# A vision tower's last layer and first patch blocks as whole fp32 products on one Trainium2 core

## The reference, cut to what matters

```python
h = tok(x)                                   # patches @ W_lin.T + b, class token, positions
h = h + attention(layernorm(h))              # 16 heads of 64, relative position bias
h = h + moe(layernorm(h))                    # top 2 of 7 routed experts and a shared one, hidden 1024
# L1 attn: delta = sigmoid(s @ Wd.T + bd); value = s @ Wv.T + bv
#          state = (1 - delta) * state + delta * value, over the tokens
h = h + scan(layernorm(h))
# L1 ffn:  xr, xk = mixes of a token and the one before it
#          sigmoid(xr @ Wr) * (relu(xk @ Wk) ** 2 @ Wv)
h = h + rwkv_ffn(layernorm(h))
```

## Time and profile before

| | us |
|---|---|
| median of 3 runs (340.35 to 342.18) | 340.74 |
| the profiled execution's own time | 340.65 |
| its span | 338.6 |
| TensorE busy | 324.1 |
| VectorE busy | 216.9 |
| ScalarE busy | 197.8 |
| GpSimd busy | 144.5 |
| DMA, mean over the span | 131 GB/s |

### The profile page before, as it was taken

One profiled execution on the slowest core, in us unless ns is written; L12 is line 12 of the kernel. 1 busy time (PEld: TensorE's weight loads), 2 busy tenths in 40 slices (PEclk: granted clock), 3 DMA queues, 4 the chain that ended last, 5 costly groups with the idle time before them and its releaser, 6 DMA issues.

```text
span 338.6 us, 7784 instructions
## 1 busy us (share of the span) xinstructions
PE 324.1 (96%) x3308; PEld 304.6 (90%) x3308; DVE 216.9 (64%) x379; ACT 197.8 (58%) x332; POOL 144.5 (43%) x101
## 2 busy tenths in 40 slices
PE   8999999999999999999999989999999999989875
PEld 8976877899998999999999989999999999968765
DVE  2667233555564587678839685766757688736884
ACT  4772333755645685457687456656566566537681
POOL 3143012385442323548374365665665874000231
PEclk9999999999999999999999999999999999999999
DMA  7937450003000521568756456464758351000002
GB/s 275 407 124 221 136 200 0 6 2 128 4 2 4 186 64 65 188 204 282 220 184 189 120 212 208 153 214 155 217 162 293 135 155 53 1 5 2 1 0 73
DMA packets 30499, 44.43 MB, mean 131 GB/s; under 512 B 1586, under 2 KB 19314, under 8 KB 30332
## 3 DMA queue, kind: packets, MB, share of 16 engines
q1 hardware_dynamic: 27868, 39.89, 35.8%
q0 software_dynamic: 960, 2.43, 2.3%
q10 hardware_dynamic: 1632, 1.57, 1.4%
HBM read 38.22 MB, written 5.49 MB: 129 GB/s over the span
## 4 chain that ended last, share of the span: by engine, by line
PE 78%; DVE 11%; ACT 6%; issue 2%; DMA 1%; POOL 1%; ACTq 0%; SPq 0%; DVEq 0%
PE ps L1498 21%; PE ps L1500 20%; PE ps L1499 20%; DVE c_region L937 3%; PE ps L1530 3%; PE ps L1630 3%; PE ps L1657 2%; DVE w_lo L937 2%; PE ps L1523 2%; PE ps L1615 1%; DMA v_region<-in_patches 1%; ACT w_hi L637 1%; DVE s_region L1275 1%; DVE xn_lo L937 1%; PE ps L1547 1%
## 5 line engine op out<-in xcount | busy, mean ns | idle before, releaser
L1498 PE MATMUL ps<-c_region,w_hi 128*128 128x256 f32 (+2 forms) x320 | 95.2, 297 | 2.8 <-DVE c_region L937 1.5
L1500 PE MATMUL ps<-c_region,w_lo 128*128 128x256 f32 (+2 forms) x320 | 92.1, 288 | 0.0
L1499 PE MATMUL ps<-c_region,w_hi 128*128 128x256 f32 (+2 forms) x320 | 92.0, 288 | 0.0
L1498 PEld LDWEIGHTS ps<-c_region,w_hi 128*128 128x128 f32 x320 | 61.1, 191 | 4.5 <-DVE c_region L937 2.7
L402 POOL TENSOR_TENSOR w_lo<-w_stage,w_hi 128x1024 fp32r<-128x1024 f32 x15 | 44.7, 2981 | 45.1 <-ACT w_hi L637 45.0
L1499 PEld LDWEIGHTS ps<-c_region,w_hi 128*128 128x128 f32 x320 | 61.1, 191 | 0.2
L1500 PEld LDWEIGHTS ps<-c_region,w_lo 128*128 128x128 f32 x320 | 61.0, 191 | 0.0
L937 DVE TENSOR_TENSOR c_region<-s_region,c_region 128x512 fp32r<-128x512 f32 (+1 forms) x44 | 47.9, 1088 | 18.1 <-ACT c_region L772 12.6
L637 ACT ACTIVATE w_hi<-w_stage 128x1024 fp32r<-128x1024 f32 (+1 forms) x42 | 49.6, 1192 | 4.4 <-DVE v_region L1330 4.4
L1498 PE MATMUL ps<-xn_hi,w_hi 128*128 128x296 f32 x152 | 47.7, 314 | 1.1 <-DVE xn_lo L937 1.1
L1499 PE MATMUL ps<-xn_lo,w_hi 128*128 128x296 f32 x152 | 45.4, 299 | 0.0
(11 more groups left out here) (185 smaller groups left out, 637.1 us busy)
## 6 DMA issues: line engine op xcount, KB each, us to landing
w_stage<-in_w_gate SPq DMA_DIRECT2D x17, 512.0 KB, 4.2
w_stage<-in_w_up SPq DMA_DIRECT2D x17, 512.0 KB, 4.2
w_stage<-in_w_down SPq DMA_DIRECT2D x8, 1024.0 KB, 5.5
expert_rows<-zeros SPq DMA_DIRECT2D x1, 1792.0 KB, 13.8
v_region<-in_patches SPq DMA_DIRECT2D x3, 576.0 KB, 5.7
v_region<-expert_rows SPq DMA_DIRECT2D x1, 1536.0 KB, 7.2
expert_out<-v_region ACTq DMA_DIRECT2D x6, 256.0 KB, 3.9
v_region<-in_w_l SPq DMA_DIRECT2D x1, 1280.0 KB, 6.8
```

The lines of the kernel that those rows point to most:

```text
L1498: mm(o, a_h, b_h, start=start, stop=False)
L1499: mm(o, a_h, b_l, start=False, stop=False)
L1500: return mm(o, a_l, b_h, start=False, stop=stop)
```

## The change

- Patches and W_lin come as six blocks, one transfer each. Blocks 0 and 1 go to TensorE as they are, in one fp32 product instead of three; blocks 2 to 5 are split as before. TensorE begins with 5 zero products instead of 15.
- 16 of the 37 bias products stand between the mean and the variance of the first norm, 21 behind it. They use banks 5 and 7.
- `value(0, 0)` becomes `value_full(0, 0)`: two fp32 products of 512 columns. The load of w_o, which goes over w_v, waits for them.
- ScalarE casts w_k behind the first half's `high`, and w_q behind the second half's.
- `token_weights` and `choice_weights` stand behind expert 2's last copy.
- The last layers' weights are not split: they are loaded into the staging tile, and every product of those layers is one fp32 product (`full`). The casts and subtractions of their weights and inputs are gone.
- TensorE's list of the last layers stands within both branches (`last_layer`). 13 zero products are left out there (4, 7 and 2).

```diff
-            for i in range(3):
-                for o, x, n in ((wlin_s, w_lin, KF * D // 3), (patch_s, patches, PW // 3)):
-                    sp.dma_start(o[:, i * n:(i + 1) * n], x[:, i * n:(i + 1) * n]).then_inc(d_patch[i], 16)
+            for k in range(KF):
+                r = slice(k * FB, (k + 1) * FB)
+                sp.dma_start(vreg[:, r], blocks[:, r]).then_inc(d_patch[k], 16)
             sp.dma_start(pb[:], par).then_inc(s["d_par"], 16)
...
             sp.dma_start(part(2).rearrange("p (k n) -> p k n", k=HP), rows(w_o, HP)).then_inc(d_w[2], 16)
...
-            sp.wait_ge(s["xg_mm"], E - 1)
-            sp.dma_start(l1_s, w_l1).then_inc(s["d_l1"], 16)
+            sp.wait_ge(lo_e["g1"], NX)
+            sp.wait_ge(lo_e["u1"], NX)
+            sp.dma_start(pat(ws[:], L1AT[0], [HID, 4], [1, KD * D]),
+                         w_l1[:, 0:4 * KD * D].rearrange("p (i n) -> p i n", i=4)).then_inc(s["d_l1"], 16)
             reload("dn", NX, KH // 2)
+            sp.dma_start(ws[:, 2 * W1 + KH // 2 * D:2 * W1 + KH // 2 * D + KD * D],
+                         w_l1[:, 4 * KD * D:L1W]).then_inc(s["d_l1"], 16)
             for c in range(C):
                 sp.wait_ge(s["out_ok"] if c else s["out0_ok"], KD)
...
-            g.memset(zero[:], 0.0).then_inc(s["const_set"], 1)
             g.memset(eps[:], EPS).then_inc(s["const_set"], 1)
             for a in (xnf, xh, xl):
...
-                act.wait_ge(d_patch[i], 32)
-                for k in (2 * i, 2 * i + 1):
-                    for o, x, n in ((wh, wlin_s, D), (patch_h, patch_s, B * NP)):
-                        a.activation(o[:, k * n:(k + 1) * n], x[:, k * n:(k + 1) * n], ACT.Copy).then_inc(s["tok_hi"], 1)
+            for k in range(FULL, KF):
+                act.wait_ge(d_patch[k], 16)
+                for o, x, n in ((wh, wlin_s(k), D), (patch_h, patch_s(k), B * NP)):
+                    a.activation(o[:, k * n:(k + 1) * n], x, ACT.Copy).then_inc(s["tok_hi"], 1)
...
-            w_high(1, W1)
...
+                act.wait_ge(d_w[1], 16)
+                w_high(1, W1)
+                high(L, 1)
                 act.wait_ge(d_w[0], 16)
                 act.wait_ge(s["tok_mm"], 4)
                 w_high(0, W1)
-                high(L, 1)
...
             root(2, 0)
-            high(2, 0)
             square(2, 1)
             root(2, 1)
             sigmoid_tables()
-            high(2, 1)
...
-                    act.wait_ge(s["ra_mm"], 2 * i + 1)
+                    act.wait_ge(s["ra_mm"], 4 * c + m + 1)
...
-            act.wait_ge(s["l1_lo"], 5)
             previous(0)
             square(3, 1)
-            mix_high(0, 1, 2)
             root(3, 1)
-            mix_high(0, 0, 4)
+            relu_first(0)
             previous(1)
-            relu_first(0)
-            mix_high(1, 1, 6)
-            relu_high(0)
-            mix_high(1, 0, 8)
             sigmoid_tables()
             receptance(0)
             relu_first(1)
-            relu_high(1)
             receptance(1)
...
-            for k in range(KF):
...
+            for k in range(FULL, KF):
...
                     gate(3)
-                    if e == 2:
-                        token_weights()
-                        dve.wait_ge(s["comb_set"], 2)
-                        choice_weights()
...
                     v.tensor_copy(y_s[:, o:o + D], bank(5, D)).then_inc(s["y_ok"], 1)
+                    if e == 2:
+                        token_weights()
+                        dve.wait_ge(s["comb_set"], 2)
+                        choice_weights()
...
             centre(2, 1)
-            low(2, 0)
             normal(2, 1)
-            low(2, 1)
...
             def relu_square(c):
                 dve.wait_ge(s["k_relu"], c + 1)
+                dve.wait_ge(s["mix_ok"], 4 * c + 4)
                 v.tensor_tensor(chunk(tmp[4], c), chunk(tmp[1], c), chunk(tmp[1], c), ALU.mult).then_inc(s["k_sq"], 1)
...
             link(inject(0))
-            v.memset(pat(xnf[:], 0, [T + 1, KD * B]), 0.0)
             link(states(0))
             add_states(0)
             link(inject(1))
+            v.memset(pat(xnf[:], 0, [T + 1, KD * B]), 0.0)
...
-            pe.wait_ge(s["const_set"], 3)
-            keep_clock(15)
-            for k in range(KF):
-                pe.wait_ge(s["tok_lo"], 2 * k + 2)
+            pe.wait_ge(s["const_set"], 1)
+            keep_clock(5)
+            for k in range(FULL):
+                pe.wait_ge(d_patch[k], 16)
+                for i, (m, c) in enumerate(MC):
+                    mm(bank(4 + i, NPC), wlin_s(k)[:, m * P:(m + 1) * P], patch_s(k)[:, c * NPC:(c + 1) * NPC],
+                       start=(k == 0), stop=False)
+            for k in range(FULL, KF):
+                pe.wait_ge(s["tok_lo"], 2 * (k - FULL) + 2)
                 for i, (m, c) in enumerate(MC):
                     w_ = slice(k * D + m * P, k * D + (m + 1) * P)
                     x_ = slice(k * NP * B + c * NPC, k * NP * B + (c + 1) * NPC)
                     w = three(bank(4 + i, NPC), wh[:, w_], wl[:, w_], patch_h[:, x_], patch_l[:, x_],
-                              k == 0, k == KF - 1)
+                              False, k == KF - 1)
                     if k == KF - 1:
                         w.then_inc(s["tok_mm"], 1)
...
-                mean(L, 0)
-                mean(L, 1)
-                variance(L, 0)
-                variance(L, 1)
-
+            def bias_columns(k0, k1):
+                for k in range(k0, k1):
+                    lhs = cb[0:BUCKETS, CB_OH + T - 1 - k:CB_OH + 2 * T - 1 - k]
+                    w = mm(ps[0:T, 5 + 2 * (k // 32), (k % 32) * HEADS:(k % 32 + 1) * HEADS], lhs, tb[0:BUCKETS, :],
+                           start=True, stop=True)
+                return w
+            pe.wait_ge(s["const_set"], 3)
             pe.wait_ge(s["cls_set"], 1)
-            norm(0)
-
+            mean(0, 0)
+            mean(0, 1)
             pe.wait_ge(s["d_const"], 16)
             pe.wait_ge(s["d_table"], 16)
-            for k in range(T):
-                lhs = cb[0:BUCKETS, CB_OH + T - 1 - k:CB_OH + 2 * T - 1 - k]
-                w = mm(ps[0:T, 1 + 2 * (k // 32), (k % 32) * HEADS:(k % 32 + 1) * HEADS], lhs, tb[0:BUCKETS, :],
-                       start=True, stop=True)
-            w.then_inc(s["bias_mm"], 1)
-
-            pe.wait_ge(w_lo[2], 1)
-            pe.wait_ge(s["up_lo"], 1)
+            bias_columns(0, 16)
+            variance(0, 0)
+            variance(0, 1)
+            bias_columns(16, T).then_inc(s["bias_mm"], 1)
+            def value_full(pair, n):
+                i = pair // 2 * 4 + pair % 2
+                for k in range(KD):
+                    w = mm(ps[0:VR, v_bank(pair, n), :], xnf[:, k * NT + i * T:k * NT + i * T + VR],
+                           ws[:, 2 * W1 + k * INNER + n * 512:2 * W1 + k * INNER + (n + 1) * 512],
+                           start=(k == 0), stop=(k == KD - 1))
+                w.then_inc(s["v_mm"], 1)
             def value(pair, n):
-                if pair == 0 and n == 1:
-                    pe.wait_ge(s["bias_ev"], 2)
...
+            pe.wait_ge(d_w[2], 16)
+            pe.wait_ge(s["ln_xn"], 1)
...
+            pe.wait_ge(w_lo[2], 1)
+            pe.wait_ge(s["up_lo"], 1)
             pe.wait_ge(s["ln_lo"], 1)
             for pair in range(PPC):
...
+                    if pair + n > 0:
+                        value(pair, n)
             pe.wait_ge(s["ln_lo"], 2)
+            pe.wait_ge(s["bias_ev"], 2)
             def project(hp, c, j):
...
                 down(e, 14)
                 down(e, 15)
+            def full(o, w_i, m, x, o0, width):
+                for k in range(KD):
+                    w = mm(o, last_w(w_i, k, m), x[:, k * width + o0:k * width + o0 + NC],
+                           start=(k == 0), stop=(k == KD - 1))
+                return w
+            def gates(c, w_i):
+                pe.wait_ge(s["ln_xn"], 5 + c)
+                for m in range(KD):
+                    i = KD * c + m
+                    full(bank(i + 4 * (w_i == 0), NC), w_i, m, xnf, c * NC, NT).then_inc(s["ra_mm"], 1)
+            def project(c, w_i, x, mixed):
+                pe.wait_ge(s["mix_ok"], mixed)
+                for m in range(KD):
+                    b = KD * c + m + (4 if w_i == 2 else 0)
+                    full(bank(b, NC), w_i, m, x, c * NC, N).then_inc(s["rk_mm"], 1)
+            def values(c):
+                pe.wait_ge(s["k_sq"], c + 1)
+                for m in range(KD):
+                    full(bank(KD * c + m, NC), 4, m, tmp[4], c * NC, N).then_inc(s["vv_mm"], 1)
+            def last_layer():
+                pe.wait_ge(s["b_mul"], BACK)
+                mean(2, 1)
+                pe.wait_ge(s["d_l1"], 32)
+                gates(0, 0)
+                variance(2, 1)
+                gates(0, 1)
+                gates(1, 0)
+                gates(1, 1)
+                mean(3, 0)
+                keep_clock(6, 1)
+                variance(3, 0)
```

(83 more changed lines are left out.)

76 lines of the change are left out of this document (19 added, 57 removed).

## The result

The change makes the kernel 0.5% faster: 339.4 us in the median against 340.89 for the kernel before (six runs each), a ratio of 0.9952 with a 95% interval of 0.9931 to 0.9972. Timed again beside three experiments it gave 0.9949 (0.9930 to 0.9967). The prediction was 336.6. The direction was right, the size was not: 4.1 us were forecast, 1.5 came. The time lies at the upper end of the stated range (333.5 to 339.5), and in the class "within 0.5%", which had a chance of 0.11.

What follows compares the result with a forecast made beforehand. TensorE, busy 324.1 of the span's 338.6 us, was taken to set the end. From 340.65: start through values 1.0 later, expert 2 1.8 and last layers 3.2 earlier, so 336.6 us; range 333.5 to 339.5.

Steps and rivals of the forecast that it cites:

- within 0.5%: Outcome class for the whole kernel: a time within 0.5% (1.7 us) of the kernel before; chance 0.11.
- 1. The blocks: Start of the kernel: with the clock rising at 5.9 us again, the last token product is out at 15.2, 1.6 earlier.
- Rival A: Start: the clock rises later, after a gap behind the zero products; 1.5 to 1.7 us more, 338.3; chance 0.15.
- 2. The norm and the values: First norm to values: TensorE waits for VectorE and goes on at 33.2, using up the start's gain; net 1.0 us later.
- The port: At the values: GpSimd's and VectorE's subtractions go one after the other, used without a gap, 2.35 us per weight step.
- the stop: At the values, near 29.5 us: TensorE stands 3.7 us waiting for VectorE, the longest stop of the program.
- Rival B: At the values: the clock falls while TensorE waits, products behind run at half pace, losing 2.35 us, 339.0; chance 0.12.
- 3. Expert 2: Experts 2 and 3: two TensorE waits, 0.51 and 1.11 us, go; gain 1.8, bounds 0.5 and 1.9.
- 4. The last layers: End of the kernel: gain 3.2 us, 1.9 from an earlier start and 1.3 from fp32 products without casts and subtractions.
- The reason given for the earlier mean: Third norm: TensorE stood 1.59 us behind the branch, then multiplied zeros; within the branch the mean starts at 299.6.
- rival E: First 40 us: the clock rises late and falls again in the wait; 1.5 + 2.35 gives 340.4, slower cases 341.7; chance 0.05.
- faster: Outcome class for the whole kernel: a time under 339.0 us; chance 0.85.

## Why the prediction was wrong, point by point

**1. The blocks: forecast 1.6 earlier, measured 0.2.** This is the step that failed first. "If the clock rises at 5.9 again" took one trace's moment for a property of the kernel. It is not even one of the changed kernel. In the seven profiles with 5 zero products, a gap and then block 0, the rise came 3.0 to 6.0 us behind block 0's first product, at 7.3 to 10.4. In the five with products from 0.98 on and next to no gap it came 3.6 to 5.8 behind the first of them, at 4.6 to 6.7 us. Rival A had the mechanism and the price (1.5 to 1.7; 1.4 came, of which some 0.15 is block 0's later arrival) with a chance of 0.15. The row that spoke for it was in the text: before, the rise followed 4.7 us without a gap.

**2. The norm and the values: forecast 2.6 later, measured 3.8.** The port was right. The first half was normalised at 22.40, 5.8 behind the end of the token products (5.7), the fp32 products of 512 columns took 0.86 each, VectorE's copy came behind GpSimd's second subtraction, and TensorE went on 17.6 behind (18.0). What was left out of the forecast is the clock behind the stop: 1.6 us. Rival B named it and priced it at 2.35. It had a chance of 0.12 although the stop was to be the longest of the program; the statement of the Trainium skill ("TensorE: Matmul & The Clock Gate", the part on the HAM clock gate) that idling brings the throttled clock back, put beside B there, is borne out by the five profiles with the stop (granted clock 0.50 behind it).

**3. Expert 2: forecast 1.8, measured 2.1.** Both waits are gone, and taking them back costs 2.5 in the medians.

**4. The last layers: forecast 3.2, measured 2.55.** The mean starts 1.56 earlier against the last product, the sigmoids 0.4 more, the last variance 0.2 more, and the stretch from there to VectorE's last addition is 1.36 shorter (forecast 1.3 for it). That makes 3.5 (3.2 forecast). The failed term is one that wasn't in the sum: the output's way out, 1.0 longer. A misreading had no weight: the mean of before started at 301.23 by the timeline, and 301.40 is where the chain enters it. The reason given for the earlier mean was wrong in part as well: it was less the branch than the zero products behind it. What fp32 alone is worth in these layers was not isolated.

**The sum.** In spans: 3.6 later for 1 and 2, 2.1 and 2.55 earlier for 3 and 4, 1.1 in all. Of the 2.9 us between that and the forecast's 4.0, 1.4 are the blocks (the late rise above all), 1.6 the fall, 1.0 the output; 0.3 each in 2 and 3 and 0.35 in 4 went the other way, to within the rounding. The rivals A and B, each with the rest of the forecast intact, came together. The text had that case, as the first half of rival E: both go wrong in the first 40 us, for 1.5 + 2.35 and a time of 340.4. What came is this, at 1.4 + 1.6, but it had a chance of 0.05 at most, since E also held the slower cases. (The chances named for "faster" add up to 0.89, not to the 0.85 that the text gives.) That 339.4 is still inside the range owes something to luck: the 1.0 of the output had no place in the text, and the 0.95 won in 2, 3 and 4 beyond the forecast made up for it.

## What to carry to other kernels

A clock transition seen in one trace is a draw from a spread of microseconds, not a constant: price the work near it at both levels, and give the case that rise and fall both go wrong a real chance: here each of the two new gaps brought one of them. Before moving a cast or subtraction, look which engines' port phase it lands in; here one cast moved by 7.5 us cost 3.1 us of waiting and 1.6 us of clock in the profiles, and moving it back with three more zero products and the tail behind the branch gave 7.9 us over the kernel before instead of 1.5. Follow the sum to the last byte: code moved into a branch changed how long the output took.

## What the hardware showed that I had not expected

- The clock's rise varied from 3.0 to 6.0 us behind the first real product in kernels whose first 10 us are the same code.
- A stop of 2.8 to 2.9 us was enough for the clock to fall behind it, in five of five profiles of kernels that have it; in the profile with twelve zero products in it, and in that with 24, the clock stayed at 1.00.
- A load of instructions 0.9 to 1.5 us behind the start of the last addition goes with a wait for the output that is 0.9 to 1.7 us longer, in eight of eight profiles.
- The extra gaps near 150 us in the four profiles from one chip, and in none from the others. No run looked into them.
